# A two-layer hybrid block: VectorE's order in the projections, the gate product's place, and the last coupling sums in PSUM

## What is computed

```python
x = x + attn_a(layernorm(x))   # 16 heads, 4 key heads, softmax
x = x + ffn(layernorm(x))      # 3 coupling cycles
x = x + attn_b(layernorm(x))   # rotary, causal, no softmax, then
                               # out * sigmoid(x @ Wg1 @ Wg2), norm, @ Wo
x = x + ffn(layernorm(x))      # the same weights again
```

```python
coupling = 0.1 + adaptive_range * (0.7 * gf + 0.3 * tf - 0.5) * 2.0
out = out + coupling * twist(out)    # [p_r, -p_i, -o_r, o_i]
```

## Time and profile before

| what | value |
|---|---|
| median of 3 runs | 2197.43 us |
| the profiled execution, its own time | 2189.54 us |
| its span | 2187.7 us |
| granted TensorE clock, mean over the span | 0.973 |
| TensorE busy | 2085.6 us, 95% |
| VectorE busy | 1784.7 us, 82% |
| ScalarE busy | 1478.1 us, 68% |
| GpSimd busy | 140.7 us, 6% |

### The profile page before, as it was taken

How to read it: one execution, slowest core, us unless ns; L and a number is a source line. 1 busy time by engine, 2 the same in 40 slices (tenths; PEclk the granted TensorE clock), 3 DMA queues, 4 the chain that set the end, 5 groups by cost and what they waited for, 6 DMA issues and landing times.

```text
span 2187.7 us, 48018 instructions
## 1 busy us (share of the span) xinstructions
PE 2085.6 (95%) x14214; PEld 857.4 (39%) x14214; DVE 1784.7 (82%) x3349; ACT 1478.1 (68%) x2899; POOL 140.7 (6%) x210
## 2 busy tenths in 40 slices
PE   6899999999999999999999999898997999998997
PEld 3423333333333333333333333254434555555433
DVE  5689999999999999999999999644537677776255
ACT  4438888888888888888888888744556434446653
POOL 2350000000000000000000000010002000002000
PEclk9779999999999999999999999999997999999998
DMA  6421121121121221221221221230000000000002
GB/s 165 129 69 42 45 74 48 48 75 42 52 72 41 56 68 41 62 63 41 63 61 41 66 58 42 74 102 26 1 0 1 1 0 1 1 0 1 0 0 77
DMA packets 93686, 101.19 MB, mean 46 GB/s; under 512 B 35712, under 2 KB 74896, under 8 KB 93552
## 3 DMA queue, kind: packets, MB, share of 16 engines
q1 hardware_dynamic: 93552, 99.79, 16.8%
HBM read 78.72 MB, written 20.71 MB: 45 GB/s over the span
## 4 chain that ended last, share of the span: by engine, by line
PE 86%; DVE 6%; issue 3%; ACT 3%; DMA 1%; SPq 0%; ACTq 0%; POOL 0%; DVEq 0%; POOLq 0%
PE ps L613 22%; PE ps L587 14%; PE ps L636 10%; PE ps L642 10%; PE ps L743 8%; PE ps L751 4%; PE ps L553 3%; PE ps L819 2%; PE ps L828 2%; PE ps L848 2%; PE ps L602 1%; ACT YT L1001 1%; PE ps L764 1%; PE ps L532 1%; PE ps L867 1%
## 5 line engine op out<-in xcount | busy, mean ns | idle before, releaser
L1298 DVE TENSOR_REDUCE mx<-ps 128x1 f32<-128x512 f32 x2048 | 1279.4, 683 | 23.5 <-PE ps L587 18.8
L1001 ACT ACTIVATE YT<-ps 128x512 f32<-128x512 f32 x2048 | 1058.0, 606 | 273.8 <-PE ps L642 273.7
L613 PE MATMUL ps<-YT,work 128*32 128x512 f32 x4096 | 546.1, 605 | 0.0
L587 PE MATMUL ps<-work 64*128 64x512 bf16 x2048 | 461.3, 389 | 7.5 <-DVE mx L1298 6.9
L636 PE MATMUL ps<-work 64*128 64x512 bf16 x2048 | 406.0, 378 | 2.8
L642 PE MATMUL ps<-work 34*128 34x512 bf16 x2048 | 400.6, 378 | 0.0
L587 PEld LDWEIGHTS ps<-work 64*128 64x128 bf16 x2048 | 144.6, 93 | 613.0 <-DVE mx L1298 541.6
L636 PEld LDWEIGHTS ps<-work 64*128 64x128 bf16 x2048 | 162.0, 94 | 110.5 <-ACT YT L1001 36.3
L743 PE MATMUL ps<-YT,c_s 128*128 128x512 f32 x384 | 176.6, 603 | 3.2 <-ACT work L1050 2.5
L613 PEld LDWEIGHTS ps<-YT,work 128*32 128x32 f32 x4096 | 80.7, 108 | 123.0 <-issue 86.9
L642 PEld LDWEIGHTS ps<-work 34*128 34x128 bf16 x2048 | 101.1, 94 | 49.6 <-issue 1.7
(11 more groups left out here) (142 smaller groups left out, 1670.2 us busy)
## 6 DMA issues: line engine op xcount, KB each, us to landing
work<-k_scr SPq DMA_DIRECT2D x640, 64.0 KB, 2.2
work<-q_scr SPq DMA_DIRECT2D x640, 32.0 KB, 1.8
o_scr<-o_sb SPq DMA_DIRECT2D x32, 256.0 KB, 2.1
X<-in_L_attn_a_x_dram SPq DMA_DIRECT2D x8, 512.0 KB, 7.3
work<-negt SPq DMA_DIRECT2D x256, 1.0 KB
work<-o_scr SPq DMA_DIRECT2D x16, 256.0 KB
work<-inv_scr SPq DMA_DIRECT2D x16, 256.0 KB
out_dram<-X SPq DMA_DIRECT2D x16, 256.0 KB, 2.2
```

Source lines behind the costliest of these rows:

```text
L587: mm(ps[:, bank_of[x], :], qa[rows, p, jp, qt * P:(qt + 1) * P], ka[rows, p, kc_ * CH:(kc_ + 1) * CH], start=True, stop=True).then_inc(a_m ...
L613: m = mm(ps[32 * j:32 * j + 32, 7, :], vst[:, p, t, :], prob(GROUP * t + j), start=t == 0, stop=t == KTILES - 1)
L1001: fn(prob(u), ps[:, S_BANK + u % S_RING, :], ACT.Exp, scale=HD ** -0.5).then_inc(exp_ok, 1)
L1298: dve.tensor_reduce(mx[:, p, at_:at_ + 1], ps[:, bank_of[x], :], AX_X, ALU.max).then_inc(a_max, 1)
```

## The change

1. In the loop over chunks 0 to 5, VectorE does `scaled` and `moments_of` ahead of `residue`, `put_values` and `low`, no longer between `put_values` and `low`.
2. The gate product goes from the first ffn's begin to the place between the 16 products made ahead and `step(0, 0)`; TensorE waits there until ScalarE has copied it (`w_gs`).
3. `scaled(1, 0)` and `scaled(1, 1)` go into the loop that finishes the first sub-layer.
4. For chunks 2 to 7 of the third cycle, `update` makes only the two products, into `tw` or (chunks 4 and 5) into two chunks of `th` each. `rejoin` then makes each 128 x 128 tile by two accumulating products, of `YT` with the identity and of the product's tile with the identity or with `minus`, which VectorE makes once at the start.

```diff
             for c in range(FREE):
-                residue(c)
-                put_values(c)
-                if c + 2 < NCH:
-                    scaled(0, c + 2)
+                scaled(0, c + 2)
                 if c + 3 < NCH:
                     dve.wait_ge(x_ld[c + 3], 16)
                     moments_of(0, c + 3)
+                residue(c)
+                put_values(c)
                 low(c)
...
+            dve.tensor_scalar(minus[:], ident[:], -1.0, None, ALU.mult).then_inc(c_neg, 1)
...
             for x in range(AHEAD):
                 max_mm(0, 1, x)
+            pe.wait_ge(w_ld, 16 * len(weights))
+            gate_turn()
+            gate_product()
             pe.wait_ge(n_y, 2 * NCH)
...
+            pe.wait_ge(w_gs, KT)
             step(0, 0, 2, before=False)
...
                     turn_chunk(st, 0)
-                    pe.wait_ge(w_ld, 16 * len(weights))
-                    gate_turn()
                     turn_chunk(st, 1)
-                    gate_product()
+                    pe.wait_ge(o_res, NCH - 1)
...
                     moments_of(1, c - 1)
+                if 2 <= c < 4:
+                    scaled(1, c - 2)
             add_attention(NCH - 2)
             moments_of(1, NCH - 2)
-            for c in range(3):
-                scaled(1, c)
+            scaled(1, 2)
...
-                            m = pe.transpose(ps[:, 5 + h, (t % 2) * DIM + kt * P:(t % 2) * DIM + (kt + 1) * P],
-                                             YT[:, kt, tok:tok + P], ident[:])
+                            to = ps[:, 5 + h, (t % 2) * DIM + kt * P:(t % 2) * DIM + (kt + 1) * P]
+                            if c < 2:
+                                m = pe.transpose(to, YT[:, kt, tok:tok + P], ident[:])
+                            else:
+                                mm(to, YT[:, kt, tok:tok + P], ident[:], start=True, stop=False)
+                                m = mm(to, turned_by(c)[:, kt, t * P:(t + 1) * P], (ident, minus)[kt][:], start=False, stop=True)
...
+                    if n >= FN - NCH + 2:
+                        to = turned_by(c)
+                        if c < 4:
+                            dve.wait_ge(f_up, base + n - 1)
+                        if c >= 6:
+                            dve.wait_ge(y_tr, 2 * (k * NCH + c - 4) + 2)
+                        dve.tensor_tensor(to[:, 0, :], cs[:, c % 4, :], YT[:, 1, ch(c)], ALU.mult).then_inc(f_tw, 1)
+                        dve.tensor_tensor(to[:, 1, :], cs[:, c % 4, :], YT[:, 0, ch(c)], ALU.mult).then_inc(f_up, 1)
+                        return
```

More of the change, by code:

```diff
@@ L113, in hybrid_block @@
         head = sb("head", [P, HPK])
+        minus = sb("minus", [P, P])
         diag = sb("diag", [P, HEADS, HD])
@@ L656, in step, with gate_turn, gate_product @@
                         sums(s - 1, 1 - p, KTILES - 1)
+            def gate_turn():
+                pe.wait_ge(n_y, 2 * NCH)
+                for kt in range(KT):
+                    m = pe.transpose(ps[0:HD, 7, kt * P:(kt + 1) * P], g1_s[:, kt, :], ident[:])
+                m.then_inc(w_gt, 1)
+            def gate_product():
+                pe.wait_ge(w_ge, 1)
+                for kt in range(KT):
+                    m = mm(ps[:, 7, kt * DIM:(kt + 1) * DIM], g1_t[:, kt, :], g2_s[:], start=True, stop=True)
+                m.then_inc(w_gm, 1)
             def first_maxima(*those):
@@ L698, in _ @@
             pe.wait_ge(o_ev, STEPS)
-            def gate_turn():
-                for kt in range(KT):
-                    m = pe.transpose(ps[0:HD, 7, kt * P:(kt + 1) * P], g1_s[:, kt, :], ident[:])
-                m.then_inc(w_gt, 1)
-            def gate_product():
-                pe.wait_ge(w_ge, 1)
-                for kt in range(KT):
-                    m = mm(ps[:, 7, kt * DIM:(kt + 1) * DIM], g1_t[:, kt, :], g2_s[:], start=True, stop=True)
-                m.then_inc(w_gm, 1)
             def feed_forward(k):
@@ L985, in _ @@
                     stored(act, pt, c)
+            act.wait_ge(w_gt, 1)
+            act.copy(g1_t[:].rearrange("p k n -> p (k n)"), ps[0:HD, 7, 0:KT * P]).then_inc(w_ge, 1)
+            act.wait_ge(w_gm, 1)
+            for kt in range(KT):
+                act.copy(lvg_s[:, kt, DIM:2 * DIM], ps[:, 7, kt * DIM:(kt + 1) * DIM]).then_inc(w_gs, 1)
             def collect(s, i, p):
@@ L1021, in spread @@
                 m.then_inc(n_xn, 1)
-            def gate_rows():
-                act.wait_ge(w_gt, 1)
-                act.copy(g1_t[:].rearrange("p k n -> p (k n)"), ps[0:HD, 7, 0:KT * P]).then_inc(w_ge, 1)
-            def gate_weights():
-                act.wait_ge(w_gm, 1)
-                for kt in range(KT):
-                    act.copy(lvg_s[:, kt, DIM:2 * DIM], ps[:, 7, kt * DIM:(kt + 1) * DIM]).then_inc(w_gs, 1)
             def feed_forward(k):
```

15 lines of the change are left out of this document (8 added, 7 removed).

## The result

The changed kernel takes **2187.72 us** (median of 5 runs, 2183.43 to 2189.67) against 2197.04 for the kernel before on the same chip (5 runs, 2195.67 to 2198.44). The ratio is 0.9955, with an interval of 0.9941 to 0.9970: 9.3 us by the medians, 0.45% faster, and clear of no change. The forecast was 2192.2 in a range of 2186.5 to 2198.5. The time is in the range; the sum of -5.2 was 4 us too small, and two of its terms are not what I thought.

A forecast was written before the change was run, and what follows sets the result against it. TensorE was taken as the bound, 95% busy, with VectorE close behind in the steps. Terms -12.0 + 3.0 - 4.5 + 6.1 + 2.2 gave -5.2 us, from 2197.4 to 2192.2, range 2186.5 to 2198.5.

The forecast's parts named there:

- leaves the steps as they are: Steps: TensorE has no gap there, 180.8 of 181 us busy, so the change can only move what lies around them.
- Part 1, -12.0: Projections: VectorE's new order shortens chunks 4 and 5 to 8.05 us rounds; first maximum from 92.89 to about 80.9.
- 0.15 for `minus`: Projections, ahead of the first maximum: making `minus` on VectorE adds only 0.15 us.
- Part 2 ahead of step 0, +3.0: Ahead of step 0: gate transposes, copies and products are new work on TensorE, +3.0 us, bounds 0 and 3.9.
- 0.4 back: Ahead of step 0: VectorE catches up meanwhile, so two products behind the gate need not wait for a bank, 0.4 us.
- Parts 2 and 3 at the first ffn, -4.5: First ffn's start: turns begin at once after ScalarE's last copy, L743 at about 1481.2; -4.5 us, between -2.1 and -5.
- Part 4, +6.1 and +2.2: Ends of both ffns: 32 TensorE instructions for 8 per chunk cost +6.1 us in the second, +2.2 in the first.
- the third rival: Rejoin in both ffns: identity products do not lift the clock, which stays at half; time near 2231; chance 0.07.
- the stretch at 1680: First ffn's end: TensorE did only transposes from 1680 to 1682 and stayed at 0.50; evidence for the half-clock rival.
- the projections gain less: Rival, projections: TensorE stays at 1.2 GHz through part of chunks 4 and 5; -8 instead of -12, 2196.2; chance 0.20.
- the gate was not hidden: Rival, ahead of step 0: negated maxima's load sets the step's start, so the gate's 3 us vanish; 2189.2; chance 0.13.
- the last rival: Ffn ends: adds leave VectorE but time does not fall, as TensorE takes more than it frees; no separate chance given.

The follow-up runs named there:

- the last kernel: Changed kernel with sums in PSUM undone, VectorE's constants behind step 0's 64 maxima, gate product back in first ffn, three ScalarE copies instead: 2169.62 us, ratio 0.9888.

## Why the prediction was right, and where not

**What bounds the kernel: right in TensorE and VectorE, wrong in "leaves the steps as they are".** I had looked at a stretch of 181 us as a sum (180.8 busy) and so could not see that ScalarE starts late once in two steps. The late start shows in TensorE's rows only as products that stand longer. It gave -6.9 in the profiles (-5.3 in 13 turns, the rest in the last stretch, which varies), more than the whole sum I forecast.

**Part 1, -12.0 (bounds -3 to -13).** The mechanism was right up to the last `residue`: the stores hold chunks 2 and 3, the rounds are 8 us, TensorE keeps up. (The working itself, redone, ends at 81.1 and not 80.9: it leaves out the other constants, 0.76, and with the 0.3 of `moments_of` it is 81.4.) Alone it took 9.0 off the first maximum and 11.6 off the time (by the interval 7.5 to 16); with the constants moved as well, in the last kernel, it took 13.6 off the first maximum. In the change it is -6.6. The step that failed is "0.15 for `minus`", with "POOL's two memsets ... end before POOL's part for chunk 6 is due": I asked who waits for the memsets, not whom they hold. (They did move, too: the first starts at 78.87 and not at 81.13.) Moving VectorE's constants 11 us forward laid them beside the memsets, and `minus` made the last copy miss the gap between the two: 5.07 for 0.76. Another 1.5 is the later stores.

**Part 2 ahead of step 0, +3.0.** The profile pair has +2.45, the averages +3.6, in part a longer time at half clock. The upper bound of 3.9, every part at 1.2 GHz, is what ran; the "0.4 back" did not come, as VectorE lost 3.66 there.

**Parts 2 and 3 at the first ffn, -4.5.** Measured -4.40, 1.25 of it by the gate and 3.15 by the rows that are ready.

**Part 4, +6.1 and +2.2.** Measured +6.4 (less 0.17 behind it), and +2.9 to the last product of the first end; the table load behind the rows that the +2.2 was worked out for comes 34.4 us behind the first product of `rejoin(2)` and not 32.1: +2.3. The price of 0.112 per instruction was right: 32 of them follow in 3.57. The half clock for 3.7 us and no longer was right as well, so the third rival is out: the clock rose while TensorE did products with the identity. But that isn't their merit. Transposes alone did the same in the kernel before, windows of its second end (columns as in the earlier trace rows):

```profile
2167.60:2171.00 3.40, 3.37 (x16) 2.52 (x14) 2.59 (x5) 1.06 (x2) 0.00 (x0) 0.50 0.32 105
...
2172.00:2174.00 2.00, 0.97 (x8) 0.84 (x8) 2.00 (x5) 0.00 (x0) 0.00 (x0) 1.00 0.09 30
```

Behind 3.7 us of nothing but transposes without a gap, the next eight ran at a granted clock of 1.00, 1.16 us for all. With TensorE idle for 2.04 us ahead of these eight and for 2.57 us behind them, waiting for VectorE, the clock then fell to 0.50 again. The sixteen from 2180.49 on, 3.90 us without a gap and with only transposes for 13 us before them, were followed by 1.00 too, from 2184.7. The other kernels without part 4 show the same rise at the first place. So in these rows the waits go with the half clock and not the kind of work, and the stretch at 1680 that spoke for the rival had the same end: the clock rose at 1682.9. The sentence of the Trainium skill (TensorE: Matmul & The Clock Gate, Part 4: PE-mode transpose) that the prediction leans on, by which transposes don't count for the clock as other matmuls do, does not fit these rows, and the rows decide.

Not in the sum was the 3.7 that `minus` costs in the projections; with it, the marks give 3.2 + 6.5 + 3.7 = 13 us for part 4. By the times its price is less sure: 0.9955 or 0.9965 against 0.9933 are 5 to 7 us, while the version with the constants moved as well lies 17 below the changed kernel.

**The sum.** By the profiles the stretches with an edit, and the steps, give -6.56 + 2.45 - 6.87 - 4.40 + 2.87 + 6.40 - 0.17 = -6.3, against -9.3 by the medians and -5.2 forecast. That the forecast lay so near is luck in part: 5.4 too much in part 1 and 6.9 not seen in the steps nearly cancel. Of the rivals, "the projections gain less" came true in its size (-8 or less) and not in its cause; the gate was not hidden. What stood under the last rival (without parts 1 to 3 "slower by 8.3") was measured with part 3 left in, as +5.5, and parts 1 to 3 without part 4, with the constants later, are the better kernel.

## What to carry to other kernels

When work is moved earlier, look at what the other engines do at its new time, not only at who waits for it: on VectorE a copy of 0.2 us took 3.6 beside a GpSimd memset, while reductions ran untouched. An exchange of VectorE's time for TensorE's pays only where VectorE is what the end waits for; here 24 operations of 0.6 us were saved by 288 more instructions. And compare a loop's periods one by one: a pause at its turn is invisible in a sum, and it moves when instructions are added ahead of the loop.

## What the runs showed of the hardware that I had not expected

A loop's turn costs ScalarE a pause of 1.5 to 1.6 us or of 1.1 to 1.2 in the mean of 13 turns (0.42 at the group before, mostly), by how many instructions of its own lie ahead. One ahead gives a pause of 1.3 and no shorter period: with 0 or 1 the periods of two collected copies at a turn average 41.2 to 41.4, with 3 they average 40.8 to 40.9, and with 8 the same, but with 0.1 more in the other step. A memset of 2 x 4096 bf16 takes GpSimd 3.5 us, and VectorE's copies and scalings of 64 or 128 columns wait for its end, while operations of one column at 0.13 and maxima at 0.62 run beside it. Transposes alone, 3.7 us without a gap, were followed by the full clock just as products were. And a stretch with the same code on TensorE and ScalarE (G to H) came out as 164.5, 165.2, 167.4 or 169.0 in one kernel's profile or another's, by how long TensorE stood at half clock at its start, so a pair of profiles can't tell 4 us apart, and the stretches without an edit have to be taken out first.
